# One pass of the image-pair pipeline in another order: TensorE's turns, ScalarE's norm and ReLU, and the group sums' bank

## The reference, cut to what matters

```python
x = x + L0(_gn(x), ...)   # _gn: mean and variance over pairs of channels (32 groups), no scale
x = x + L1(_gn(x), masks, conv_w, gamma, beta)

L0: four parallel 3x3 convolutions of sign(x) with sign(w1) -> batch norm -> relu (only its sign matters)
    -> four 3x3 convolutions with sign(w2) -> batch norm -> sum over the four, weighted by lambdas
    -> relu(sum + input)
L1: mid = x * resized mask;  attention = sigmoid(conv7x7([mean_c mid, max_c mid, mask]))
    out = mid * attention;   relu(5 * (instance norm(out) * gamma + beta))
```

## Time and profile before

| | |
|---|---|
| median of 3 runs | 236.1 us (233.74 to 237.11) |
| the profiled execution's own time | 235.81 us |
| its span in the trace | 234.0 us |
| TensorE busy | 200.6 us, 86% |
| ScalarE busy | 175.0 us, 75% |
| VectorE busy | 167.7 us, 72% |
| GpSimd busy | 157.3 us, 67% |

### The profile page before, as it was taken

One profiled execution on the slowest core, in us unless ns is written; L12 is line 12 of the kernel. 1 busy time (PEld: TensorE's weight loads), 2 busy tenths in 40 slices (PEclk: granted clock), 3 DMA queues, 4 the chain that ended last, 5 costly groups with the idle time before them and its releaser, 6 DMA issues.

```text
span 234.0 us, 8993 instructions
## 1 busy us (share of the span) xinstructions
PE 200.6 (86%) x3807; PEld 125.8 (54%) x3807; DVE 167.7 (72%) x434; ACT 175.0 (75%) x230; POOL 157.3 (67%) x217
## 2 busy tenths in 40 slices
PE   8998996679899989989799979997999798997800
PEld 3556553355566556645565556565656564566800
DVE  2677265746765698967967799868576956998873
ACT  2687669827968798878879897989798978531491
POOL 8533552053534697769786988798859887854990
PEclk9999999979999999999999999999999999999955
DMA  6898000670405440652135213521352136306035
GB/s 217 294 272 312 14 4 20 190 222 8 137 3 172 110 140 4 183 167 70 73 130 149 82 62 118 166 71 73 110 172 78 67 123 157 117 27 210 0 137 206
DMA packets 12429, 28.48 MB, mean 122 GB/s; under 512 B 2293, under 2 KB 4213, under 8 KB 12389
## 3 DMA queue, kind: packets, MB, share of 16 engines
q1 hardware_dynamic: 11653, 26.84, 37.0%
q10 hardware_dynamic: 736, 1.06, 1.3%
HBM read 21.29 MB, written 6.61 MB: 119 GB/s over the span
## 4 chain that ended last, share of the span: by engine, by line
PE 28%; DVE 18%; ACT 15%; POOL 15%; issue 11%; DMA 9%; SPq 2%; DVEq 0%; POOLq 0%; ACTq 0%
DMA att_b<-attention_rows 8%; PE c L997 8%; PE c L1015 5%; POOL o L416 5%; POOL o L429 4%; DVE ve L770 4%; POOL X L434 4%; PE small L1076 4%; PE small L1084 4%; DVE bnst L738 3%; PE small L1064 3%; ACT word L582 3%; ACT S L597 3%; PE y L1039 3%; DVE red L817 3%
## 5 line engine op out<-in xcount | busy, mean ns | idle before, releaser
L1015 PE MATMUL c<-S,w2t 64*32 64x392 f16 x2304 | 55.2, 331 | 2.1 <-DVE RD L798 2.1
L997 PE MATMUL c<-E,w1t 64*128 64x420 f16 (+1 forms) x576 | 54.6, 331 | 1.2 <-ACT E L576 0.7
L798 DVE SCALAR_TENSOR_TENSOR RD<-RD,c 128x784 f16<-128x784 f16 x32 | 30.5, 955 | 27.4 <-ACT RD L604 27.4
L738 DVE BATCH_NORM_STATS2 bnst<-X 128x6 f32<-128x392 f32 x64 | 32.6, 551 | 21.4 <-POOL X L434 18.4
L1015 PEld LDWEIGHTS c<-S,w2t 64*32 64x32 f16 x2304 | 30.8, 92 | 21.3 <-issue 8.1
L1064 PE MATMUL small<-cs,o 128*112 128x130 f32 x196 | 30.0, 296 | 10.4 <-DVE red L819 5.7
L997 PEld LDWEIGHTS c<-E,w1t 64*128 64x128 f16 x576 | 25.7, 94 | 23.2 <-issue 4.3
L416 POOL TENSOR_TENSOR o<-o,mask_b 128x784 f32<-128x784 f32 x14 | 26.1, 1863 | 17.5 <-ACT o L626 10.8
L582 ACT ACTIVATE word<-c 128x840 int32<-128x840 f32 (+1 forms) x32 | 26.1, 816 | 13.9 <-PE c L997 13.7
L1064 PEld LDWEIGHTS small<-cs,o 128*112 128x112 f32 x196 | 24.4, 184 | 16.0 <-DVE red L819 7.7
L592 ACT ACTIVATE S<-word,thr_high 128x840 f16<-128x840 int16 (+1 forms) x32 | 30.6, 957 | 1.1
(11 more groups left out here) (134 smaller groups left out, 279.5 us busy)
## 6 DMA issues: line engine op xcount, KB each, us to landing
X<-in_x SPq DMA_DIRECT2D x16, 392.0 KB, 6.0
mask_b<-mask_rows SPq DMA_DIRECT2D x32, 196.0 KB, 3.4
out<-o SPq DMA_DIRECT2D x15, 392.0 KB, 3.8
att_b<-attention_rows SPq DMA_DIRECT2D x28, 196.0 KB, 5.0
o<-in_w ACTq DMA_DIRECT2D x1, 576.0 KB, 5.0
o<-in_masks SPq DMA_DIRECT2D x1, 512.0 KB, 7.6
band<-in_band SPq DMA_DIRECT2D x1, 441.0 KB, 10.2
cs<-in_cst SPq DMA_DIRECT2D x1, 434.0 KB, 4.5
```

Of the source, the lines that this page charges most:

```text
L738: dve.bn_stats(bnst[:, n, t, i, :], src[:, HALF * i:HALF * (i + 1)]).then_inc(stats[n], 1)
L798: dve.scalar_tensor_tensor(RD[:, hh, 1, :], RD[:, hh, 0, :], -IMG / TINY, second_sums(), ALU.mult, ALU.add).then_inc(low2, 1)
L997: mm = pe.matmul(c1[:, 512 - n * (1 - i):512 + n * i], w1t[64 * i:64 * i + 64, s, :], window(START[i][hh], ROWS[hh], s, E[64 * i:64 * i + ...
L1015: mm = pe.matmul(c2[at:at + Q32, LOW + HALF * i:LOW + HALF * (i + 1)], w2t[64 * r:64 * r + 64, s, q, :], window(RH * half_of(i, hh), RH, s ...
```

## The change

- TensorE: conv1(k,1) goes ahead of turn chunks 0 and 1 of k-3, and conv2(k,0) ahead of group_2(k-2) and turn chunk 2.
- The group sums of the second norm go to a corner of the bank small[1], in which chunks 0 and 2 of the turn also land, in place of the first columns of y; so `mix(t,1)` has no wait on var2 any more, while `group_2` waits for the reduced chunk 0 of pair k-3, and `terms2` for its turned chunk 2.
- ScalarE: words1(k,0) ahead of relu_block(k-2); high_sums(k-1,1) ahead of the gates (k,0); last_relu(k-6) from the middle of the pass to behind high_sums(k,0), just ahead of normalise2(k-2).
- VectorE: low_sums(k-1,1) ahead of stats_x1(k-2); the term variance + eps is written to PSUM beside the group sums and read from there by one scalar_tensor_tensor for each pair, where batches of several pairs took two tensor_tensor.

```diff
--- before.py
+++ after.py
@@ -114,12 +114,12 @@
         bnst = sb("bnst", [P, 3, NT, 2, 6], F32)
         mv = sb("mv", [P, 3, NT, 2], F32)
         dm = sb("dm", [P, 2, NT], F32)
-        veps = sb("veps", [P, 2, NT], F32)
+
         nm1 = sb("nm1", [P, NT], F32)
         ve1 = sb("ve1", [P, NT], F32)
         r1 = sb("r1", [P, NT], F32)
         nmr1 = sb("nmr1", [P, NT], F32)
-        dm2 = sb("dm2", [P, NT], F32)
+
         b1 = sb("b1", [P, NT], F32)
         nm2 = sb("nm2", [P, NT], F32)
         ve2 = sb("ve2", [P, NT], F32)
@@ -221,8 +221,11 @@
             at = padded[:, PW + 1:PW + 1 + (H - 1) * PW + W]
             return bass.AP(at.tensor, at.offset, [list(at.ap[0]), [PW, H], [1, W]])
 
-        def group_at(t):
-            return small[1][:, AT_GROUP:AT_GROUP + 2 * t]
+        def group_at(t, m=2):
+            return small[1][:, AT_GROUP:AT_GROUP + m * t]
+
+        def group2_at(t, m=2):
+            return y[:, 0:m] if t >= POOL_X else small[1][:, AT_GROUP + 12:AT_GROUP + 12 + m]
 
 
         x_in = [sem(f"x_in{t}") for t in range(NT)]
@@ -247,7 +250,7 @@
         steps1, steps2 = sem("steps1"), sem("steps2")
         var1, var2 = sem("var1"), sem("var2")
         rstd1, rstd2, shift2 = sem("rstd1"), sem("rstd2"), sem("shift2")
-        bias1, shift1, square1 = sem("bias1"), sem("shift1"), sem("square1")
+        bias1, shift1 = sem("bias1"), sem("shift1")
         signed = sem("signed")
         conv1_done, worded1, gated_low, gated_high = (
             sem(n) for n in ("conv1_done", "worded1", "gated_low", "gated_high"))
@@ -700,21 +703,21 @@
                                    scale=sc3[:, t:t + 1]).then_inc(relu_half, 1)
 
             for k in range(1, NT):
+                words1(k, 0)
                 relu_block(k - 2)
-                words1(k, 0)
-                high_gates(k, 0)
-                low_gates(k, 0)
                 if k == 1:
                     keep_mask_h()
                 high_sums(k - 1, 1)
+                high_gates(k, 0)
+                low_gates(k, 0)
                 sign_x(k + 1)
                 if k == 1:
                     keep_mask_w()
-                last_relu(k - 6)
                 words1(k, 1)
                 high_gates(k, 1)
                 low_gates(k, 1)
                 high_sums(k, 0)
+                last_relu(k - 6)
                 normalise2(k - 2)
                 sigmoid(k - 3)
 
@@ -761,18 +764,15 @@
                     stats_of(t, 2, o[:, t, :])
 
             def group_terms(n, a, z, nm, ve, mean, chain, count, var):
-                ps = (group_at(z - a) if n == 0 else y[:, 0:2]).rearrange("p (t m) -> p m t", m=2)
+                ps = (group_at(z - a, 3) if n == 0 else group2_at(a, 3)).rearrange("p (m t) -> p m t", m=3)
                 dve.tensor_scalar(nm[:, a:z], ps[:, 0, :], -1.0, None, ALU.mult).then_inc(mean, 1)
-                dve.tensor_scalar(veps[:, n, a:z], ps[:, 1, :], EPS, None, ALU.add).then_inc(chain, 1)
+                dve.tensor_scalar(ps[:, 2, :], ps[:, 1, :], EPS, None, ALU.add).then_inc(chain, 1)
                 dve.tensor_tensor(dm[:, n, a:z], mv[:, n, a:z, 0], ps[:, 0, :], ALU.subtract).then_inc(chain, 1)
                 dve.wait_ge(chain, 2 * count)
-                if z - a == 1:
-                    dve.scalar_tensor_tensor(ve[:, a:z], dm[:, n, a:z], dm[:, n, a:z], veps[:, n, a:z],
-                                             ALU.mult, ALU.add).then_inc(var, 1)
-                    return
-                dve.tensor_tensor(dm2[:, a:z], dm[:, n, a:z], dm[:, n, a:z], ALU.mult).then_inc(square1, 1)
-                dve.wait_ge(square1, count - 3)
-                dve.tensor_tensor(ve[:, a:z], dm2[:, a:z], veps[:, n, a:z], ALU.add).then_inc(var, 1)
+                for t in range(a, z):
+                    last = dve.scalar_tensor_tensor(ve[:, t:t + 1], dm[:, n, t:t + 1], dm[:, n, t:t + 1],
+                                                    ps[:, 2, t - a:t - a + 1], ALU.mult, ALU.add)
+                last.then_inc(var, 1)
 
             def terms1(n):
                 dve.wait_ge(group1, n + 1)
@@ -781,6 +781,8 @@
             def terms2(t):
                 if has(t):
                     dve.wait_ge(group2, t + 1)
+                    if 0 < t < POOL_X:
+                        dve.wait_ge(turned, turn_count(t - 1, 2))
                     group_terms(1, t, t + 1, nm2, ve2, mean2, steps2, t + 1, var2)
 
             def make_bias1(n):
@@ -922,8 +924,8 @@
                     stats_x(t)
                 if k in TERMS_AT:
                     make_bias1(TERMS_AT[k])
+                low_sums(k - 1, 1)
                 stats_x1(k - 2)
-                low_sums(k - 1, 1)
                 reduce_chunks(k - 3, 0)
                 reduce_chunks(k - 3, 1)
                 terms2(k - 2)
@@ -969,17 +971,22 @@
                 wait(pe, var1, n)
                 if n > 2:
                     wait(pe, pooled, 3 * (next(k for k in TERMS_AT if TERMS_AT[k] == n) - 3))
-                pe.matmul(group_at(z - a), cs[:, K_PAIR:K_PAIR + P],
-                          mv[:, 0, a:z, :].rearrange("p t m -> p (t m)"), start=True, stop=True).then_inc(group1, 1)
+                pe.matmul(group_at(z - a).rearrange("p (m t) -> p m t", m=2), cs[:, K_PAIR:K_PAIR + P],
+                          mv[:, 0, a:z, :].rearrange("p t m -> p m t"), start=True, stop=True).then_inc(group1, 1)
 
             def group_2(t):
                 if not has(t):
                     return
                 pe.wait_ge(local[1], t + 1)
-                wait(pe, y_added, t + 1 if t < NT - 2 else NT)
+                if t < POOL_X:
+                    pe.wait_ge(var1, 2 + sum(t + 2 >= k for k in TERMS_AT))
+                    if t > 0:
+                        pe.wait_ge(pooled, turn_count(t - 1, 0))
+                else:
+                    pe.wait_ge(y_added, NT)
                 if t == NT - 1:
                     pe.wait_ge(var2, t)
-                pe.matmul(y[:, 0:2], cs[:, K_PAIR:K_PAIR + P], mv[:, 1, t, :], start=True, stop=True)\
+                pe.matmul(group2_at(t), cs[:, K_PAIR:K_PAIR + P], mv[:, 1, t, :], start=True, stop=True)\
                   .then_inc(group2, 1)
 
             def window(row0, rows, s, src):
@@ -1024,10 +1031,6 @@
                 pe.wait_ge(low2, 2 * t + hh + 1)
                 if hh == 0:
                     wait(pe, y_added, t)
-                elif t < NT - 1:
-                    wait(pe, var2, t)
-                else:
-                    pe.wait_ge(var2, NT - 2)
                 if t == 0 and hh == 0:
                     pe.wait_ge(mix_ready, 1)
                     pe.wait_ge(beta_ready, 1)
@@ -1162,16 +1165,16 @@
                 mix(k - 1, 0)
                 if k == 1:
                     resize_mask_w()
+                conv1(k, 1)
                 if k == 3:
                     pe.wait_ge(mask_rows, 2)
                 turn(k - 3, 0)
                 turn(k - 3, 1)
-                conv1(k, 1)
                 if k == 2:
                     turn_mask()
+                conv2(k, 0)
                 group_2(k - 2)
                 turn(k - 3, 2)
-                conv2(k, 0)
                 mix(k - 1, 1)
                 attention(k - 3)
                 if k + 1 in TERMS_AT and TERMS_AT[k + 1] > 2:
```

## The result

The changed kernel takes 246.44 us (245.56 to 247.2, four runs) against 236.61 of the kernel before in the same session: a ratio of 1.047, 95% interval 1.042 to 1.053. It is slower by 9.8 us; forecast were 14.8, and 250.6 us. The profiled execution's span grew from 234.0 to 244.3 us.

What follows compares the result with a forecast made beforehand. No engine was full, so the order of waits was taken as the bound. Costs of 13.7 (ten passes), 0.8 (early passes) and 0.3 (tail) sum to 14.8; 235.81 + 14.8 = 250.6 us, range 244 to 256.5.

Steps and rivals of the forecast that it cites:

- part 1: last_relu just ahead of normalise2: ScalarE idles 2.89 us a pass while GpSimd does last_sum and power2; cost 13.7 us.
- rival C: Passes 1 to 5 come 2.8 us earlier and nothing is lost in passes 7 and 11: 245.2 us; chance 0.14.
- Ten passes: normalise2 of pass 5 to pass 15: 10 x 13.06 + 1.8 = 132.4 us, against 118.74 before.
- The price of 3.92: Per pass, start of last_relu to start of normalise2: last_relu 1.03, then 0.08, 1.96 last_sum to power2, 0.85 to normalise2.
- Passes 7 and 11: low_sums stands behind make_bias1, which waits for power1 of four pairs; conv2 ends 0.9 us late in each, 1.8 in all.
- part 2: The other moves, seen in passes 1 to 5: normalise2 of pass 5 at 80.2 us, not 79.44, so +0.8.
- part 4: The tail, behind normalise2 of pass 15 to the span's end: 35.8 us before, +0.3 us after the change.
- part 3: Variance with a PSUM operand, group sums in the other bank: variance takes 0.222 us, off the path after pass 5, worth 0.
- rival B: The old chain of waits stays the bound, the round trip costs nothing, shorter variances save 10.9 us: 225 us; chance 0.03.
- the ring: Chain of waits repeating every 23.52 us before: variance, power, normalise2, make_u, attention rows' DMA, GpSimd and VectorE to the next variance.
- A: TensorE idles 2.3 us in odd passes, the slow clock comes in, conv2 up to 1 us late in five: 255.6 us; chance 0.12.
- D: The step acts as said, but in fewer passes or with partial cover: within 2%, 231 to 241 us; chance 0.05.

Runs made afterwards that it cites:

- e1: The changed kernel with last_relu(k-6) alone put back between sign_x and words1(k,1); 234.74 us, ratio 1.000 to the kernel before.
- e5: The changed kernel with GpSimd's last_sum adding x over only the first 392 of 784 columns; 238.45 us, ratio 1.012 to the kernel before.
- e12: The changed kernel with 20 idle matmuls on TensorE ahead of conv1(k,1) in even passes from 8 on; 246.99 us, ratio 1.055 to the kernel before.
- e6: The changed kernel with the variance's operand back in SBUF, group sums staying in their new place; 247.4 us, ratio 1.050 to the kernel before.
- e2: The kernel before with last_relu(k-6) alone moved to just ahead of normalise2; 271.5 us, ratio 1.156 to the kernel before.
- e3: The changed kernel with power2(k-2) ahead of last_sum(k-6) in GpSimd's list; 240.33 us, ratio 1.022 to the kernel before.
- e4: The kernel before with only the variance's operand put in PSUM, batches by single instructions; 232.54 us, ratio 0.991 to the kernel before.
- e9: The kernel before with last_relu just ahead of normalise2 and conv2(k,0) ahead of group_2 and turn chunk 2; 264.63 us, ratio 1.129.
- e8: The kernel of e7 with last_relu(k-6) one place later, behind words1(k,1); 231.8 us, ratio 0.985 to the kernel before.
- e7: The kernel of e1 with pass 1's gates back ahead of mask copy and high_sums, keep_mask_rows back ahead of terms2(0); 233.84 us, ratio 0.996.
- e11: The kernel of e8 with power2 ahead of last_sum on GpSimd; 238.54 us, ratio 1.017 to the kernel before.

## Why the prediction was right, and where its terms were off

**The mechanism** stands: ScalarE's hole between last_relu and normalise2 (part 1). e1 removes it by one line and the loss is gone; e5 shortens one link by 0.9 us and the whole by 8; e12 and e6 leave it and the time stays. The count that led there holds too: conv2 was to end 7.0 us behind normalise2 and ScalarE to come to its high_sums at 8.4; in the pass from 117.95 they measure 7.04 and 8.39. What the prediction didn't see is that the same move costs about three times as much in the old order (e2), where conv2 comes later.

The measured loss, 9.8 us, is under the forecast 14.8. The time lies in the range, but 4.2 us under 250.6 and nearer to rival C's 245.2, whose reasons didn't come in; that the range held it is in part owed to C and the margin. The terms, against the spans' 10.3:

- Ten passes: forecast 132.4 us, measured 128.88 (78.82 to 207.70). The largest miss. The price of 3.92 from last_relu to normalise2 measured 3.80 (127.04 to 130.84). I had read 1.96 from last_sum to power2 as GpSimd's own time; it measures 1.83 to 1.86. In the kernel before the variance beside that last_sum ended only with it:

```profile
125.32 1.29 DVE L770 SCALAR_TENSOR_TENSOR ve<-dm,veps 128x1 f32<-128x1 f32 x1
```

So power2 there waited for 126.61, not for last_sum alone. Another 0.1 a pass lies in the starts of ScalarE's other instructions. Together 0.2 to 0.3 a pass, some 2.5 us. And pass 15 has no sign_x, since there is no pair 16: 12.03 us, 0.8 less, which I overlooked.
- Passes 7 and 11: forecast 0.9 more each, measured 13.70 against 12.8. Right.
- Passes 1 to 5 (part 2): forecast +0.8, measured 78.82 - 79.44 = -0.6. The mask rows did come late, but the first make_u started at 47.08, not 48.0, and the first twelve turns ran at full clock in the profiled execution, 1.55 us, where before they took 2.91. In e1, e5 and e6 the same turns took 2.91 again and the conv2 behind them 3.0 to 3.1 in place of 1.72, and normalise2 of pass 5 came at 80.8 to 81.2; in e3 and e12, where only one of the two was slow, at 79.3 and 79.4. e2, whose passes 1 to 5 are those of the kernel before, had its turns at 1.55 too and came to 78.25. So the term depends on the clock in that execution: with those turns at full clock the new order is 0.6 us later, near the forecast, and -0.6 comes from comparing a fast stretch with a slow one.
- The tail (part 4): forecast +0.3, measured 36.6 against 35.8 = +0.8. TensorE stood idle for 3.70 us ahead of the last pair's turns and ran them slow, 2.94 us. But e6 has the same tail of 36.6 us with these turns at 1.58 (the matmuls that spread the attention over the channels behind them took 5.6 us in place of 4.8). So the slow turns alone don't explain it, and the cause of the 0.5 over the forecast stays open (first line the changed kernel, second e6):

```profile
211.31 2.94 PE L1067 MATMUL small<-cs,o 128*112 128x130 f32 x12 [3.70 <-POOL o L419]
```

```profile
213.59 1.58 PE L1072 MATMUL small<-cs,o 128*112 128x130 f32 x12 [3.28 <-POOL o L421]
```

- The variance (part 3): worth 0 in the changed order, as I took it (e6). No run takes the new bank of the group sums by itself; e1 has it, together with all other moves but last_relu's, at 1.000. The rule of the Trainium skill ("SBUF — State Buffer", section "Who interferes with whom"), that a VectorE instruction with at most one SBUF input doesn't contend with GpSimd, agrees with e4: with the PSUM operand no variance is longer than 0.217 us, also beside a last_sum. The excess did go, and the whole came down by 2 us of rival B's 10.9, since the earlier trace rows's DMA and GpSimd's sums close the ring almost as late. The unknown price of VectorE's write to PSUM is 0.157 us, against 0.151 to SBUF.

Of the rivals, A came half true: ahead of conv1(k,1) TensorE idles for 2.15 us (forecast 2.3) in pass 10 and 2.14 in pass 14, but only 1.24 and 1.25 in passes 8 and 12. The clock drops behind it in pass 10 (0.71 over 5 us, 18 matmuls in 2.92 us) and not in pass 14 (1.60). The drop costs 0.1 us: pass 10 takes 12.82 us, and 12.72 in e12, where the clock stayed up. conv2(10,0) ends at 139.10, just ahead of ScalarE's high_sums (139.17). My estimate of up to 1 us each in five passes was wrong. B, C and D didn't come in.

What stays open: how the 19 us of e9 over the changed kernel divide between low_sums, conv1's place, ScalarE's other moves and the sums' bank.

## What to carry to other kernels

When an instruction is moved next to another of its own engine, look into the other engine's list for what stands between the two: an unmoved last_sum ahead of power2 turned two independent steps of ScalarE into a round trip over GpSimd of 2.8 us a pass. The cover for such a trip must lie between release and wait. In the changed kernel a pass took ScalarE's work plus what wasn't covered; in e8, with up to 1.07 us uncovered, the passes were shorter than in e7 all the same, so an exposed wait is a loss only where it closes the ring. What one late step costs depends on how long the ring is that it lands in (37 us in the old order, 11 in the new), so take single moves of a change apart in both directions.

## What the runs showed that I had not expected

- An idle of 2.15 us of TensorE was followed by the slow clock and one of 2.14 was not, in one and the same execution; after 3.40 us idle the turns ran at full clock once and took 2.91 us after 3.42 in another. The length of the idle alone didn't tell.
- The long variances of the kernel before also go without the PSUM operand, by an order in which GpSimd has no last_sum running then (e6: 355 ns at most on that line).
- Doing the awaited step first on GpSimd made things slower (e11 against e8, 7.6 us); GpSimd then waited for the variance with a last_sum undone behind it.
